# Wo, scaled by the first tanh factor, and its two products placed ahead of the first keys of a one-core gated cross-attention and expert kernel

## What is computed

```python
x = x + tanh(g_xattn) * attention(k=ctx, v=ctx, q=layernorm(x))   # Wq, bq, Wk, Wv, bv, Wo, bo
n = layernorm(x)
shared = (silu(n @ w1) * (n @ w2)) @ w3
scores = sigmoid(n @ router_w); top 2 of scores + expert_bias
routed = sum over the two of score * swiglu_expert(n)
x = x + tanh(g_ffn) * (shared + routed)
```

## Time and profile before

| | us |
|---|---|
| runs | 62.84, 64.78, 64.87; median 64.78 |
| the profiled execution | 63.06 |
| its span, first to last instruction | 61.1 |
| TensorE busy (matmul) | 54.5 (89%) |
| VectorE busy | 41.0 (67%) |
| ScalarE busy | 23.9 (39%) |
| GpSimd busy | 19.2 (31%) |
| mean granted TensorE clock | 0.988 of full |

### The profile page before, as it was taken

How to read it: one execution, slowest core, us unless ns; L and a number is a source line. 1 busy time by engine, 2 the same in 40 slices (tenths; PEclk the granted TensorE clock), 3 DMA queues, 4 the chain that set the end, 5 groups by cost and what they waited for, 6 DMA issues and landing times.

```text
span 61.1 us, 1244 instructions
## 1 busy us (share of the span) xinstructions
PE 54.5 (89%) x356; PEld 47.5 (78%) x356; DVE 41.0 (67%) x171; ACT 23.9 (39%) x72; POOL 19.2 (31%) x43
## 2 busy tenths in 40 slices
PE   0996899999999999999999999999999999999200
PEld 0355598797989999994999999999999999898000
DVE  3036989999884978222499789944877647887600
ACT  0522748868897232246423123322223332222000
POOL 4604069989109969930020550000000000000000
PEclk9999999999999999999999999999999999999995
DMA  0789981000000000000000006488850000003360
GB/s 0 194 240 274 313 357 48 0 0 0 0 5 0 0 11 0 0 0 5 0 0 0 11 0 171 113 274 237 303 189 0 0 0 5 0 0 97 85 177 11
DMA packets 5256, 4.77 MB, mean 78 GB/s; under 512 B 384, under 2 KB 5120, under 8 KB 5248
## 3 DMA queue, kind: packets, MB, share of 16 engines
q1 hardware_dynamic: 4816, 4.33, 22.9%
q10 hardware_dynamic: 432, 0.35, 2.2%
HBM read 4.15 MB, written 0.52 MB: 76 GB/s over the span
## 4 chain that ended last, share of the span: by engine, by line
PE 67%; DVE 12%; DMA 8%; SPq 3%; issue 2%; ACT 1%; DVEq 0%
PE bank L835 17%; PE bank L836 17%; PE bank L849 12%; DMA x_sb<-in_x_dram 8%; PE bank L862 4%; PE bank L981 3%; PE bank L980 3%; PE bank L990 3%; DVE xn L515 2%; DVE final L641 2%; DVE stats L499 2%; PE bank L807 2%; SPq L253 2%; SPq L252 1%; PE bank L813 1%
## 5 line engine op out<-in xcount | busy, mean ns | idle before, releaser
L428 ACT ACTIVATE silu_t<-bank 128x256 f32<-128x256 f32 x28 | 10.8, 384 | 23.5 <-PE bank L836 19.7
L613 DVE TENSOR_TENSOR hid<-silu_t,bank 128x256 f32<-128x256 f32 x28 | 11.5, 416 | 7.6 <-ACT silu_t L428 4.1
L849 PEld LDWEIGHTS bank<-shared_sb,hid 128*128 128x128 f32 x64 | 9.4, 191 | 1.1 <-issue 0.4
L849 PE MATMUL bank<-shared_sb,hid 128*128 128x128 f32 x64 | 9.8, 277 | 0.0
L835 PE MATMUL bank<-x2nT,shared_sb 128*128 128x256 f32 x32 | 9.6, 383 | 0.0
L836 PE MATMUL bank<-x2nT,shared_sb 128*128 128x256 f32 x32 | 9.5, 379 | 0.0
L836 PEld LDWEIGHTS bank<-x2nT,shared_sb 128*128 128x128 f32 x32 | 6.1, 191 | 0.8
L862 PE MATMUL bank<-tile_w,hid 128*128 128x128 f32 x32 | 4.8, 279 | 0.1
L835 PEld LDWEIGHTS bank<-x2nT,shared_sb 128*128 128x128 f32 x32 | 4.8, 192 | 0.1
L862 PEld LDWEIGHTS bank<-tile_w,hid 128*128 128x128 f32 x32 | 4.5, 191 | 0.4 <-issue 0.2
L328 POOL TENSOR_SCALAR x2n<-x,mean_var,rstd 128x128 f32<-128x128 f32 x6 | 4.7, 796 | 0.3
(11 more groups left out here) (118 smaller groups left out, 100.5 us busy)
## 6 DMA issues: line engine op xcount, KB each, us to landing
tile_w<-in_routed_w_dram SPq DMA_DIRECT2D x10, 192.0 KB, 3.8
shared_sb<-in_shared_w_dram SPq DMA_DIRECT2D x1, 768.0 KB, 6.8
out_dram<-final SPq DMA_DIRECT2D x4, 128.0 KB, 2.2
x_sb<-in_x_dram SPq DMA_DIRECT2D x2, 128.0 KB, 4.1
ctx_sb<-in_ctx_dram SPq DMA_DIRECT2D x2, 128.0 KB, 4.1
x_sb<-in_x_dram SPq DMA_DIRECT2D x1, 256.0 KB, 5.2
ctx_sb<-in_ctx_dram SPq DMA_DIRECT2D x1, 256.0 KB, 5.5
params<-in_attn_params_dram ACTq DMA_DIRECT2D x1, 201.0 KB, 2.9
```

The source lines that it names most:

```text
L428: nc.scalar.activation(silu_t[:, k % 3, :], bank[UP_BANK[k % 3]][:, 0:256], ACT.Silu).then_inc(silu_ready, 1)
L613: nc.vector.tensor_tensor(hid[:, k % 3, :], silu_t[:, k % 3, :], bank[UP_BANK[k % 3]][:, 256:512], ALU.mult)\
L849: last = nc.tensor.matmul(dst[:, c * P:(c + 1) * P], hid[:, k % 3, i * P:(i + 1) * P], w3s[:, j, :], start=(j == 0 and c == 0), stop=(j == ...
```

## The change

The two gains get a tile and a load of their own (8 bytes for each partition), issued on ScalarE's queue between the parameters and Wo; the row parameters are loaded without them. On ScalarE tanh and woT stand ahead of copy_ctx(0), and the copy of vo_w ahead of copy_h(0). On TensorE the transpose of Wo stands ahead of turn_ctx(0), and the two products with woT (their order is swapped) ahead of keys(0); values(0) stands ahead of score(0). On VectorE bv_mat stands ahead of the wait for kq, bias_rows and maximum(0) ahead of moments_x(2).

```diff
--- before.py
+++ after.py
@@ -64,8 +64,9 @@
         wo_sb, wq_sb, wk_sb, wv_sb = (params[:, m * D:(m + 1) * D] for m in range(4))
         bq_col, bv_col = params[:, 4 * D:4 * D + 1], params[:, 4 * D + 1:4 * D + 2]
         rw_sb = params[:, 4 * D + 2:4 * D + 2 + E]
-        rows = sb("rows", [P, D + E + 2])
-        bo_rows, ebias, gains = rows[:, 0:D], rows[:, D:D + E], rows[:, D + E:D + E + 2]
+        gains = sb("gains", [P, 2])
+        rows = sb("rows", [P, D + E])
+        bo_rows, ebias = rows[:, 0:D], rows[:, D:D + E]
         shared_sb = sb("shared_sb", [P, 3 * H])
         w1s, w2s = shared_sb[:, 0:H], shared_sb[:, H:2 * H]
         w3s = shared_sb[:, 2 * H:3 * H].rearrange("p (j d) -> p j d", j=HJ)
@@ -150,6 +151,7 @@
         rest_hid = sb("rest_hid", [P, 512])
 
         params_loaded = sem("params_loaded")
+        gains_loaded = sem("gains_loaded")
         wo_loaded = sem("wo_loaded")
         rows_loaded = sem("rows_loaded")
         x_loaded = [sem(f"x_loaded{i}") for i in range(3)]
@@ -376,8 +378,9 @@
         @block.scalar
         def _(act):
             act.dma_start(params[:, D:4 * D + 2 + E], attn_params[:, D:4 * D + 2 + E]).then_inc(params_loaded, 16)
+            act.dma_start(gains[:, :], row_params[:, D + E:D + E + 2].to_broadcast([P, 2])).then_inc(gains_loaded, 16)
             act.dma_start(wo_sb, attn_params[:, 0:D]).then_inc(wo_loaded, 16)
-            act.dma_start(rows[:, :], row_params.to_broadcast([P, D + E + 2])).then_inc(rows_loaded, 16)
+            act.dma_start(rows[:, :], row_params[:, 0:D + E].to_broadcast([P, D + E])).then_inc(rows_loaded, 16)
             nc.scalar.preload_act_table(ACT.Exp)
 
             def copy_ctx(g, src):
@@ -427,16 +430,16 @@
                     act.wait_ge(hid_ready, k - 2)
                 nc.scalar.activation(silu_t[:, k % 3, :], bank[UP_BANK[k % 3]][:, 0:256], ACT.Silu).then_inc(silu_ready, 1)
 
-            copy_ctx(0, bank[1])
-            act.wait_ge(rows_loaded, 16)
-            nc.scalar.activation(tanh_g[:, :], gains, ACT.Tanh).then_inc(tanh_ready, 1)
+            act.wait_ge(gains_loaded, 16)
+            nc.scalar.activation(tanh_g[:, :], gains[:, :], ACT.Tanh).then_inc(tanh_ready, 1)
             act.wait_ge(tanh_ready, 1)
             act.wait_ge(wo_turned, 1)
             nc.scalar.mul(woT[:, :], bank[2][:, 0:D], tanh_g[:, 0:1]).then_inc(woT_ready, 1)
+            copy_ctx(0, bank[1])
+            act.wait_ge(vo_w_done, 1)
+            nc.scalar.copy(vo_w[:, :], bank[3][:, 0:D]).then_inc(vo_w_ready, 1)
             copy_h(0, bank[0])
             copy_x(0, bank[1])
-            act.wait_ge(vo_w_done, 1)
-            nc.scalar.copy(vo_w[:, :], bank[3][:, 0:D]).then_inc(vo_w_ready, 1)
             copy_ctx(1, bank[6])
             softmax(0, bank[5])
             copy_ctx(2, bank[0])
@@ -644,20 +647,21 @@
 
             dve.memset(fill[:, :], 1.0).then_inc(fill_ready, 1)
             moments_x(0)
+            dve.wait_ge(consts_ready, 2)
+            dve.wait_ge(params_loaded, 16)
+            nc.vector.tensor_scalar(bv_mat[:, :], ones_mat[:, :], bv_col, None, ALU.mult).then_inc(bv_ready, 1)
             dve.wait_ge(kq_done, 1)
             step(nc.vector.reduce_sum(kq_sum[:, :], bank[0][:, 0:D], AX))
             step(nc.vector.tensor_scalar(kq_shift[:, :], bank[0][:, D:D + 1], kq_sum[:, 0:1], SCALE / D, ALU.subtract, ALU.mult))
             nc.vector.tensor_scalar(kq[:, :], bank[0][:, 0:D], SCALE, kq_shift[:, 0:1], ALU.mult, ALU.add).then_inc(kq_ready, 1)
             normalise(0)
-            dve.wait_ge(consts_ready, 2)
-            nc.vector.tensor_scalar(bv_mat[:, :], ones_mat[:, :], bv_col, None, ALU.mult).then_inc(bv_ready, 1)
             moments_x(1)
-            moments_x(2)
-            maximum(0, bank[5])
             dve.wait_ge(bias_done, 1)
             dve.wait_ge(tanh_ready, 1)
             dve.wait_ge(rows_loaded, 16)
             nc.vector.scalar_tensor_tensor(bias_rows[:, :], bo_rows, tanh_g[:, 0:1], bank[4][:, 0:D], ALU.mult, ALU.add).then_inc(bias_ready, 1)
+            maximum(0, bank[5])
+            moments_x(2)
             moments_x(3)
             invert(0)
             copy_values(0, bank[7])
@@ -869,20 +873,20 @@
             nc.tensor.matmul(bank[0][:, 0:D], wk_sb, wq_sb, start=True, stop=True)
             nc.tensor.matmul(bank[0][:, D:D + 1], wk_sb, bq_col, start=True, stop=True).then_inc(kq_done, 1)
             pe.wait_ge(ident_ready, 1)
-            turn_ctx(0, bank[1])
             pe.wait_ge(wo_loaded, 16)
             nc.tensor.transpose(bank[2][:, 0:D], wo_sb, ident[:, :]).then_inc(wo_turned, 1)
+            turn_ctx(0, bank[1])
+            pe.wait_ge(woT_ready, 1)
+            nc.tensor.matmul(bank[3][:, 0:D], wv_sb, woT[:, :], start=True, stop=True).then_inc(vo_w_done, 1)
+            pe.wait_ge(bv_ready, 1)
+            nc.tensor.matmul(bank[4][:, 0:D], bv_mat[:, :], woT[:, :], start=True, stop=True).then_inc(bias_done, 1)
             pe.wait_ge(kq_ready, 1)
             keys(0, bank[0])
             turn_x(0, bank[1])
-            pe.wait_ge(bv_ready, 1)
-            pe.wait_ge(woT_ready, 1)
-            nc.tensor.matmul(bank[4][:, 0:D], bv_mat[:, :], woT[:, :], start=True, stop=True).then_inc(bias_done, 1)
-            nc.tensor.matmul(bank[3][:, 0:D], wv_sb, woT[:, :], start=True, stop=True).then_inc(vo_w_done, 1)
             turn_ctx(1, bank[6])
-            score(0, bank[5])
             pe.wait_ge(vo_w_ready, 1)
             values(0, bank[7])
+            score(0, bank[5])
             values(1, bank[2])
             turn_ctx(2, bank[0])
             keys(1, bank[6])
```

## The result

| | before | changed |
|---|---|---|
| runs | 20 | 20 |
| median us | 64.3 | 64.23 |
| lowest to highest us | 62.84 to 65.02 | 63.59 to 66.24 |
| profiled execution us (span) | 63.06 (61.1) | 64.21 (62.4) |

Ratio changed to before 1.0133, 95% interval 1.0096 to 1.017: slower by 1.3%, within the 2%. Each kernel's runs lie in two groups some 1.5 us apart; the ratio compares the lower groups alone, and the two medians nearly agree only because the changed kernel had more of its runs in its lower group (11 of 20, against 7).

A forecast was written before the change was run, and what follows sets the result against it. VectorE's work up to copy_h(3) was taken to set the end, with TensorE dense behind it. Loads 0, keys 0 and VectorE +0.31 gave +0.3 us on the median 64.78: 65.1 us, range 62.8 to 65.9.

The forecast's parts named there:

- the sum: Whole kernel: loads 0, keys 0, VectorE +0.31 make +0.3 us, 65.1 against the median; chance 0.43.
- What bounds the kernel: Last chain: TensorE is dense from values(3), released by copy_h(3), so the end moves by exactly what VectorE's work before moves.
- VectorE's order, +0.31: VectorE: maximum(0) waits for scores until 8.51, moments_x(3) starts at 9.66 instead of 9.35, with bias_rows' 0.25 us moved away.
- Wo and its products ahead of the keys, 0: TensorE's start: the two products mostly fit its 0.64 us wait, so keys(0) starts at 6.27 instead of 6.23, absorbed.
- cover is thin: TensorE before keys(0): each 0.1 us that Wo or gains are late beyond the slack moves keys(0) and all behind by 0.1.
- values(0) ahead of score(0): TensorE before the first scores: four passes, 7.42 to 7.86, so score(0) goes at 7.86 instead of 8.02, winning only 0.16 us.
- The loads, 0: Load queues: Wo and gains land within slack of about 0.35 and 0.9 us, SyncE's loads at most some 0.1 us later.
- The 64.6: Total if a fixed load cost of about 2 us stood in front of Wo, landing it at 6.2.
- Wo late: Rival at TensorE's start: Wo lands after 5.0 or gains after 5.1; up to +1.65 us, 66.4, half way 65.7; chance 0.17.
- The third x late: Rival at moments_x(2): x lands after 7.93, the new order gains up to 0.58 us from 8.82 on, 64.2; chance 0.25.
- GpSimd "about 0.1 us from being the next one late": GpSimd's chain to normalise(3), turn_x(3) at 14.32 just before values(3) at 14.65: charged nothing, upper end +0.1 us.
- The third rival: Whole kernel: the new runs fall into the lower group, 63.4 us with the forecast's +0.3; chance 0.15.

The follow-up runs named there:

- 1.0327: The changed kernel with moments_x(2) ahead of maximum(0) again, bias_rows still early; ratio 1.0327 to the kernel before.
- the 0.9959: The kernel before in every order, but with the gains in the parameters and no longer in the rows; ratio 0.9959 to the kernel before.
- the second comparison: The changed kernel itself run again against the kernel before: median 65.92 us, before 63.66, too few comparable runs for an interval.
- version of what helps: The kernel before with gains in the parameters, bv_mat ahead of kq, bias_rows ahead of moments_x(2), maximum(0) behind it, TensorE as before; ratio 0.9997.

## Why the prediction was right, and where its steps were not

The forecast was a small loss within 2%, 65.1 us, range 62.8 to 65.9; the median is 64.23. The loss against the kernel before is 1.3%, where the sum had 0.3 us, 0.5%. The direction and the main mechanism (VectorE idle in front of the maximum, with the statistics behind it) were right; the size is 0.8 us, 1.3% of some 63, and so more than twice the sum. That the median lies in the range says little for the sum: the range is 3.1 us wide, and a step of 0.3 us and one of 0.8 both lie in it.

Of the signs that the prediction named for being right, three came: Wo's transpose at 5.13, moments_x(2) held by its place alone, and the dense stage as long as before. woT (5.68), keys(0) (7.12), the scores (8.54), the maximum (9.29, after 1.14 us idle) and values(3) (15.38) were all later than it had them, and one of its signs for being wrong came, turn_x(3) waiting for GpSimd past 14.6 (15.13).

*What bounds the kernel.* Right, and the best part. From moments_x(3) to values(3) it was 4.99 us before, 4.94 after, and 4.90 to 4.98 in all but two of the other profiles (5.24 and 5.25, both with bias_rows and the statistics ahead of the maximum). From values(3) to the last silu it was 40.87 before and 40.99 after. Whatever moved moments_x(3) moved the last instruction. What comes behind that, the stores of the output, was taken as fixed and was not, see the last section.

*VectorE's order, +0.31.* The mechanism holds, the size does not. Its two halves, the maximum waiting for TensorE and the x already there, are shown by the run with VectorE's order alone: 0.012, or 0.74 us, give or take 0.45. The term was too small because the scores in front of the maximum were put at 8.47, from rows of a single execution; the whole kernel's slack there hangs on how soon TensorE gets through its first steps. And the 0.25 us that bias_rows gives back in that sum are not to be had in every order: with the statistics ahead of the maximum they come to nothing (last section).

*Wo and its products ahead of the keys, 0.* This is the step that failed most. It took 0.11 us for a pass, from a row at 7.80, and so 0.44 for the two products. In the trace of the kernel before these same products held TensorE for 0.52 us, 7.28 to 7.80, where turn_ctx(1) starts:

```profile
7.28 0.46 PE L880 MATMUL bank<-woT,bv_mat 128*128 128x128 f32 x2
...
7.57 0.39 PE L881 MATMUL bank<-woT,params 128*128 128x128 f32 x2
```

In the changed kernel the transpose took 0.45 (0.27 foreseen), woT came at 5.68 (5.41), and the four passes held TensorE from 6.10 to 7.12, 1.0 us. keys(0) was 0.9 us late, not 0.04. Against the 6.27 of the forecast that is 0.85 us: 0.27 because the products began later, 0.08 by the row above, and 0.5 because TensorE was at its low pace until about 7 us. That last part could not be read from the kernel before, where the low pace ended at about 5 us; it is that the end of the low pace moves from one execution to the next. The "cover is thin" was said; a price for a later rise of the pace was not.

*values(0) ahead of score(0).* The prediction charged four passes, 0.44 us. Wrong place: in the changed kernel xnT was there at 8.49, when values(0) was done (8.07 to 8.51 on TensorE, scores at 8.54), and the swap back won nothing.

*The loads, 0.* The bounds set were on when the gains and Wo land, and those were near (gains 3.2 us, Wo 3.3, so 4.96 against a need of 5.0). The load that did come late was another: the 128 small packets were charged at most 0.1 us on SyncE's queue, and the third x came 1.3 us later. In the whole change this cost little or nothing, since the new order held VectorE beyond it (9.63 against 9.26), so the 0 came out by luck; without the new orders the same load made the kernel 2.3% longer. The Trainium skill (DMA: Bandwidth & Descriptors, "Rules for kernel authors") had warned of small transfers, and the prediction set the warning aside because set-up overlapped in the trace. With that rule the trace agrees after all, not as set-up in front of Wo but as time of the DMA engines: 3.7% of them for the queue in place of 2.2%, at the same 0.35 MB. (The 64.6 that the prediction works out for a cost of 2 us in front of Wo starts from the profiled execution, 63.06; from the median, as its other prices do, the same step gives about 66.3.)

*The rivals.* Wo late: seen in the load alone (6.42) and, by 0.2 and 0.3 us, in two others, not in the changed kernel. The third x late: it came, made by the change itself, at 9.26, beyond the 8.82 at which the gain was to be full; yet the gain was not had, since the scores were late too and 8.84 in that reckoning had become 9.63. That the old order would have done worse with such loads is not settled (1.0327, with a profile that does not show it). GpSimd "about 0.1 us from being the next one late": it became the releaser of turn_x(3), and cost 0.04. The third rival came in part: the median lies below the 65.1, with 11 of 20 runs at 63.59 to 64.24.

*What the parts cost together.* The load alone 2.3%, the orders alone 1.0% (1.4% over the 0.9959 that they start from), both 1.3% at first and about 2% in the second comparison. They do not add up. Two readings are open, and no run parts them: under the new order a late x finds VectorE waiting for the scores anyway; and in the changed kernel tanh no longer waits for the rows (4.39 us, against 7.54 in the load alone), so that late rows do not make the scores late.

## What to carry to other kernels

When an engine runs a fixed list, price a swap by the arrival of both inputs: the step whose input may be late, and is not yet wanted, goes behind. For work of TensorE moved into the first microseconds, price it at both of its paces, since one trace does not tell how long the low one lasts. An operation taken off the engine that is full wins nothing if the next one there is then held by another engine; look at what ends it, not only at what starts it. And a load of a few bytes for each partition is not free because it is small; send the bytes with a load that goes anyway.

## What the runs showed of the hardware

*Small packets.* 128 packets of 8 bytes and what goes with them, 144 packets in all, raised the share of the queue from 2.2 to 2.8% (eight profiles without them) to 3.3 to 4.1% (six with them), and the third x on the other queue landed 0.7 us or more later than in any kernel without them. In which way (time for each packet, or the broadcast load behind them) no run tells.

*TensorE's pace at the start.* The profile's granted clock reads 1.00 in every stretch of the first 12 us, but the distance of passes speaks against that. Here is the kernel with VectorE's order alone:

```profile
7.33 0.63 PE L779 MATMUL bank<-ident,xn 128*128 128x128 f32 x2
7.76 0.64 PE L882 MATMUL bank<-woT,bv_mat 128*128 128x128 f32 x2
8.19 0.63 PE L883 MATMUL bank<-woT,params 128*128 128x128 f32 x2
8.61 0.64 PE L773 MATMUL bank<-ident,ctx_sb 128*128 128x128 f32 x2
...
11.25 0.38 PE L773 MATMUL bank<-ident,ctx_sb 128*128 128x128 f32 x2
11.47 0.60 PE L784 MATMUL bank<-ctxT,kq 128*128 128x256 f32 x2
```

Two passes take 0.43 us up to 8.6, and 0.22 from 11.25: the lower of the two clock levels, 1.2 GHz, then the upper, 2.4. In the kernel with the products ahead alone the passes were at the upper level from 4.4 us, in the kernel before from about 5, in the changed kernel from about 7. TensorE had run the same seven filler products ahead of each. Six of the kernels here have TensorE's list exactly as before, and in their six profiles the upper level came at 4.3, 4.8, about 5, 6, 10 and 11 us. The Trainium skill (TensorE: Matmul & The Clock Gate, "What's actually happening") has the point at which the clock rises vary from run to run for the same kernel. These traces agree that it varies, but not with the 0.5 us that the page gives for it.

*The stores at the end.* The profile counts no instruction of an engine behind the last sum of the output, and from there the span went on for 3.4 to 4.2 us in 13 profiles and for 5.3 in the one of the kernel with the products ahead alone. There the stores took 3.6 us to landing in the median (2.0 to 2.2 in 12 of the others) and the last one was issued 1.0 us after the last sum (0.2 in the kernel before). So a single time can be over a microsecond longer without anything in front of it having changed.

*GpSimd holds up a tiny operation of VectorE.* The version of what helps, and the kernel it is made from (GpSimd's xb(0) and VectorE's var_eps of 2 elements):

```profile
9.45 0.73 POOL L335 TENSOR_TENSOR xb<-x_sb,bias_rows 128x256 f32<-128x256 f32 x1
...
9.68 0.52 DVE L507 TENSOR_SCALAR var_eps<-mean_var 128x2 f32<-128x2 f32 x1
```

```profile
9.07 0.73 POOL L335 TENSOR_TENSOR xb<-x_sb,bias_rows 128x256 f32<-128x256 f32 x1
...
9.60 0.24 DVE L507 TENSOR_SCALAR var_eps<-mean_var 128x2 f32<-128x2 f32 x1
```

It takes 0.17 us when alone. Beside xb(0) it takes 0.24 or 0.52, and both times it ends as xb(0) does (9.84 and 9.80; 10.20 and 10.18). The same is seen in all seven profiles in which the two overlap, the kernel before among them (0.26 us, 10.35 and 10.32): it ends 0.02 to 0.04 us after xb(0). In the seven others it took 0.17.

This accounts for the version of what helps. The difference, 0.28 us, is just that of the two distances from moments_x(3) to values(3) (5.25 and 4.97). In both kernels xb(0) follows the inverse deviation of the third pair and so ends some 1.63 us after VectorE's var_eps of that pair starts, and the last var_eps does not end before it. Taking bias_rows from between the two only makes VectorE wait there. From var_eps of the third pair to values(3) it was 5.65 to 5.67 us in the four profiles with bias_rows between (before, gains in the parameters, products ahead alone, rows of 584 bytes), and 5.65 and 5.66 in the two without (statistics first, what helps). A version with xb(0) out of the way of that step and the statistics first was not run.

The Trainium skill (SBUF — State Buffer, "Who interferes with whom") tells of a port pair which VectorE and GpSimd share, and which one of them holds for a whole instruction while the other is blocked; the times of the trace agree. That the ports are the cause no run here shows.
